# Two gated 3x3 convolutions: the three adding groups at lags of 0, 4 and 8 units instead of 0, 6 and 12

## The reference, cut to what matters

```python
# x: (16, 64, 56, 56) float32; w_a, w_b: (64, 64, 3, 3)
def qconv_cg(x, w, theta):
    base = cin // 4                       # 16 of the 64 channels
    yp = conv3x3(x[:, :base], w[:, :base])
    yr = conv3x3(x[:, base:], w[:, base:])
    d = jax.nn.sigmoid(2.0 * (yp - theta[None, :, None, None]))
    return yp + d * yr

h = jax.nn.relu(bn(qconv_cg(x, w_a, theta_a), gamma_a, beta_a, mean_a, var_a))
h = bn(qconv_cg(h, w_b, theta_b), gamma_b, beta_b, mean_b, var_b)
return jax.nn.relu(x + h)
```

## Time and profile before

| what | value |
|---|---|
| median of 3 runs | 432.99 us (432.92 to 433.02) |
| the profiled execution | 432.81 us, of which its span is 430.7 us |
| PE (matmuls) | 424.7 us busy, 99% of the span, 9248 matmuls |
| PE weight loads | 422.8 us, 98% |
| DVE | 294.8 us, 68% |
| ACT | 257.9 us, 60% |
| granted TensorE clock | 9 tenths or more in 39 of 40 slices, 7 in the last |
| DMA | 27.77 MB, 64 GB/s mean |

### The profile page before, as it was taken

How to read it: one execution, slowest core, us unless ns; L and a number is a source line. 1 busy time by engine, 2 the same in 40 slices (tenths; PEclk the granted TensorE clock), 3 DMA queues, 4 the chain that set the end, 5 groups by cost and what they waited for, 6 DMA issues and landing times.

```text
span 430.7 us, 20664 instructions
## 1 busy us (share of the span) xinstructions
PE 424.7 (99%) x9248; PEld 422.8 (98%) x9248; DVE 294.8 (68%) x609; ACT 257.9 (60%) x507; POOL 31.5 (7%) x93
## 2 busy tenths in 40 slices
PE   9999999999999999999999999999999999999995
PEld 8999999999999999999999999999999999999994
DVE  5798665867667867666876766776766786764555
ACT  5776556655657655666665566665565765564333
POOL 6051000000000000000000000200000000000001
PEclk9999999999999999999999999999999999999997
DMA  8440116341414214151431511522515151111133
GB/s 164 91 94 9 27 27 124 65 94 29 96 41 96 56 38 96 22 113 42 85 68 23 104 29 36 112 47 56 98 24 112 40 110 34 29 22 40 38 73 76
DMA packets 120535, 27.77 MB, mean 64 GB/s; under 512 B 119936, under 2 KB 120448, under 8 KB 120448
## 3 DMA queue, kind: packets, MB, share of 16 engines
q1 hardware_dynamic: 117584, 25.87, 29.3%
q10 hardware_dynamic: 2544, 0.59, 0.6%
q0 software_dynamic: 320, 0.00, 0.0%
HBM read 13.60 MB, written 12.85 MB: 61 GB/s over the span
## 4 chain that ended last, share of the span: by engine, by line
PE 98%; DVE 1%; ACT 1%; issue 0%; DVEq 0%
PE acc L526 96%; PE acc L482 1%; PE acc L553 0%; DVE rows_out L900 0%; ACT rows_out L698 0%; DVE mix L852 0%; ACT mix L673 0%; ACT z L684 0%; DVE rows_out L939 0%; DVEq L851 0%
## 5 line engine op out<-in xcount | busy, mean ns | idle before, releaser
L526 PE MATMUL acc<-x_lo,w_hi 32*128 32x392 f32 (+1 forms) x1536 | 255.4, 336 | 0.0
L526 PE MATMUL acc<-x_hi,w_hi 32*128 32x392 f32 (+1 forms) x1536 | 255.4, 336 | 0.0
L526 PE MATMUL acc<-x_hi,w_lo 32*128 32x392 f32 (+1 forms) x1536 | 255.3, 336 | 0.0
L526 PE MATMUL acc<-h_lo,w_hi 32*128 32x398 f32 (+2 forms) x1488 | 252.3, 339 | 0.0
L526 PE MATMUL acc<-h_hi,w_hi 32*128 32x398 f32 (+2 forms) x1488 | 251.5, 338 | 0.0
L526 PE MATMUL acc<-h_hi,w_lo 32*128 32x398 f32 (+2 forms) x1488 | 251.5, 338 | 0.0
L526 PEld LDWEIGHTS acc<-x_lo,w_hi 32*128 32x128 f32 x1536 | 228.9, 183 | 0.0
L526 PEld LDWEIGHTS acc<-x_hi,w_hi 32*128 32x128 f32 x1536 | 228.7, 183 | 0.1
L526 PEld LDWEIGHTS acc<-x_hi,w_lo 32*128 32x128 f32 x1536 | 228.8, 183 | 0.0
L526 PEld LDWEIGHTS acc<-h_lo,w_hi 32*128 32x128 f32 x1488 | 220.9, 183 | 0.2
L526 PEld LDWEIGHTS acc<-h_hi,w_hi 32*128 32x128 f32 x1488 | 220.8, 183 | 0.0
(11 more groups left out here) (85 smaller groups left out, 239.4 us busy)
## 6 DMA issues: line engine op xcount, KB each, us to landing
x<-in_x_dram SPq DMA_DIRECT2D x28, 392.0 KB, 5.4
out_dram<-rows_out SPq DMA_DIRECT2D x84, 98.0 KB, 2.5
out_dram<-rows_out SPq DMA_DIRECT2D x27, 84.0 KB, 2.3
out_dram<-rows_out SPq DMA_DIRECT2D x12, 126.0 KB, 2.9
x<-in_x_dram SPq DMA_DIRECT2D x5, 98.0 KB, 3.3
x_edge<-in_x_dram SPq DMA_DIRECT2D x4, 112.0 KB, 4.7
out_dram<-rows_out SPq DMA_DIRECT2D x3, 112.0 KB, 2.3
x<-in_x_dram SPq DMA_DIRECT2D x1, 294.0 KB, 4.4
```

Source lines behind the costliest of these rows:

```text
L526: return pe.matmul(sums(bank, blk), w[g * ROWS:(g + 1) * ROWS, tap], moving(blk, part, c, dx, g), start=(u == 0 and (alone or g == bank_gr ...
```

## The change

One constant. `begins` then starts group 2's visits 4 steps after group 1's, and group 3's 8 steps after. Group 1 (lag 0) and group 0 (lag 2) keep their steps. The order of the groups at each bank stays the same.

```diff
-OFFSET = (2, 0, 6, 12)
+OFFSET = (2, 0, 4, 8)
```

## The result

| | median | range of the runs | ratio to before |
|---|---|---|---|
| before | 432.93 us (20 runs) | 432.5 to 433.2 | |
| lags 0, 4, 8 | 433.54 us (20 runs) | 433.31 to 433.71 | 1.0015 [1.0009, 1.0021] |

The change makes the kernel 0.61 us slower. The interval doesn't contain 1, but the difference is smaller than the 0.2% set beforehand as the bound, so it counts as within it. The forecast was 433.4.

The account below looks back on a forecast made before the run. PE's stream of matmul units was taken to bound the kernel; start and bank +0.77 us, steps saved at the end -0.35, together +0.42, gave 433.4 us, range 432.6 to 434.8.

Parts of the forecast that it names:

- the bank's term: Second round: block 6's first unit waits for block 1's bank until 21.50 us, making the stream 0.77 us late, start included.
- group 0's extra delay: At the start group 0 loses 0.45 us, group 1 0.27; the additional 0.18 was taken as made good.
- The rounds: Steady rounds: each takes one group's own sum, 72 units of about 0.18 us, so lags don't enter without late waits.
- The start: First units of groups 2 and 3 wait for x_hi chunks until 7.10 and 7.95 us: group 0 +0.45, group 1 +0.27.
- Parameters and block 1's bank: First round: parameters' product at step 24 comes 0.45 us later, moving the second `gated`'s end from 20.82 to 21.27 us.
- Later takeovers: Later rounds, block's first unit waiting for `gated`: four steps take 0.72 of 1.09 us room, 0.37 left, nothing lost.
- Handovers: Next group's first unit at a bank: room falls from 0.69 to 0.33 us; cost taken as 0, bounds 0 and 0.4.
- the rival of a loss in each round: Handovers of groups 2 and 3 cost in the 14 rounds with a 342-column block: 436 to 440 us, chance 0.1.
- The end: `last_base` no longer waits behind `finish(124)`: 0.35 of 0.72 us gained, then group 0's last matmul holds it.
- The cheap start: Rival at the start: waits or parameters' chain have slack, stream 0 to 0.32 us late, 432.6 to 433.0; chance 0.2.
- The case of 434.0: Rival: one-off losses, start at its upper bound 0.95 and handovers 0.4 us in rounds 2 to 6; chance 0.17.
- The strict order: Rival on PE: each unit lasts as long as its longest matmul, so fewer wide steps gain, 432.3 us; chance 0.03.

Follow-up runs that it names:

- At 3 units: Lags 0, 3 and 8 in place of the 0, 6 and 12 of the kernel before: 434.30 against 432.98 us, ratio 1.0032.
- (0, 0, 4, 8): The changed kernel (lags 0, 4, 8) with group 0 at lag 0, not 2: 433.52 us, against 432.98 for the kernel before.
- the earlier parameters: The changed kernel (lags 0, 4, 8) with the parameters' product at step 20, not 24: 433.14 us, against 432.98 for the kernel before.

## Why the prediction was right, step by step

**Forecast +0.42 us on the profiled execution, measured +0.5 of its span, +0.61 of the medians.** The sum held, its size in part by luck: the bank's term was too large and group 0's extra delay was left out, and the two errors cancel.

- *The rounds.* Forecast: the lags don't enter a round's time. The first `gated` of rounds 13, 14 and 15 are 12.98 and 12.56 us apart (191.24, 204.22, 216.78), as in the earlier trace rows within 0.04. Right.
- *The start* was about right in size. Chunks 1 and 2 were ready at 6.84 and 7.62 us, and PE's next matmuls stand at 6.90 and about 7.7, where I had 7.10 and 7.95. Of this 0.03 and 0.10 is the chunks' earlier arrival; the rest is the weight load of 0.18, which the rows don't show in full between a release and the next matmul. By the gates, the first round lost 0.28, not 0.45. That is in the main the execution's own: 12.35 to 12.43 us behind a chunk that is ready at 7.72, as in the kernel before, the gate would stand at 20.07 to 20.15, 0.38 to 0.46 late. That other groups stand behind the wait was right, as PEld shows (two loads, 0.33 us idle, released by x_hi):

```profile
6.89 0.18 PEld L526 LDWEIGHTS acc<-x_hi,w_hi 32*128 32x128 f32 x2 [0.33 <-ACT x_hi L629]
```

- *Parameters and block 1's bank.* The chain was right in each link, but moved by the smaller start: L791 came at 10.88 us where I had 11.1, the second `gated` ended at 21.02, not 21.27, and the first matmuls came at 21.17, not 21.50.
- *Group 1's step 81* was forecast 0.77 late, and from there the whole stream. Groups 1, 2 and 3 came 0.55 to 0.58 late (group 3's visits, four steps earlier, end 0.14 us sooner: 0.72 - 0.14 = 0.58). The 0.2 us too many are mostly the 0.25 by which the second `gated` ended sooner than forecast (21.02, not 21.27). The extra 0.18 of group 0, which I took as made good, mostly wasn't: group 0 is 0.86 late behind the second round and 0.74 at the end, and the end hangs on group 0. So 0.77 was right for it by luck, within the bounds of 0.32 and 0.95.
- *Later takeovers.* No recurring cost at 4, 8. The room before was not 1.09 us: in round 14 group 3's load stood at 206.75 us, where the prediction had 207.20. After, it stands at 206.61, 0.41 behind the second `gated`'s end at 206.20; one that waits stands 0.12 behind, so 0.29 us are left, where I had 0.37. The two steps from 8 to 6 are 0.36, and there the takeover waits in each of the rounds 6 to 19.
- *Handovers.* Taken as 0 at 4 units, since only a lead is lost. They do wait there, 36 of 192, and only the last round shows a loss by the gates, 0.14 us, whose cause stays open. At 3 units the room would be 3 x 0.18 - 0.39 = 0.15 us; 0.59 us are lost over 95 blocks, but two rounds in the middle still take 25.54 us. So the rival of a loss in each round had the wait right and its price wrong.
- *The end.* `last_base` was forecast at 424.27 and came at 424.23 us, directly behind group 0's last matmul; `gated(127)` at 426.05 and came at 426.11. Of the cover of 0.35 us 0.26 was gained, by the gates of blocks 126 and 127. What I missed is that group 1 and block 125 hold the same end. `finish(125)` now starts 0.71 us after `last_base`, before 0.63, so this took up to 0.08 us here; and it made the expectation for (0, 0, 4, 8) wrong.
- *The first `gated` of round 14* was forecast at 204.41 and came at 204.22 us, inside the 204.0 to 205 set for it. With the 0.58 of group 3 in place of 0.77 the sum of the prediction, 204.36 - 0.72 + 0.58, gives it.
- *The other rivals.* The cheap start (432.6 to 433.0) falls with the 0.73 us at 32.76. The case of 434.0 needed 0.4 us from handovers in rounds 2 to 6, and by the gates nothing was lost there (0.73 late behind the second round, 0.60 at block 31). The strict order would have given 432.3; the Trainium skill (TensorE: Matmul & The Clock Gate, The mechanism) has matmuls of different tiles start and end strictly in program order, and the trace after disagrees, as before. On PE near the end:

```profile
423.20 0.36 PE L526 MATMUL acc<-e_lo,w_edge_hi 32*128 32x456 f32 x1
...
423.39 0.31 PE L526 MATMUL acc<-h_lo,w_hi 32*128 32x342 f32 x1
423.41 0.37 PE L526 MATMUL acc<-e_lo,w_edge_hi 32*128 32x456 f32 x1
423.55 0.31 PE L526 MATMUL acc<-h_lo,w_hi 32*128 32x342 f32 x1
```

The group on 342 columns starts every 0.16 us (423.39, 423.55), the one on 456 every 0.21 (423.20, 423.41): each at its own pace.

What stays open is a gain from the change. With the bank's cost taken away by the earlier parameters the time is +0.16 us and not measurably under the kernel before; and no kernel here was. The wait for the chunks at the start costs more than the 0.26 us that the end gives.

## What to carry to other kernels

Tightening the stagger of a pipelined schedule pays only at its two ends, and each end has its own partner: at the front the input that the now earlier unit needs, at the back the streams that were not moved. Before shortening a lag, list for each wait behind it how late its releaser already is, in steps, and look at the first round by itself, since set-up work there makes the same wait tighter than in the steady rounds. A wait that begins to hold a unit in the middle isn't yet a cost: where groups slide against each other, it can take a lead that the next round gives back. So measure over a whole period of the schedule (here two rounds), and not over the one round that grew.

## What the runs showed of the hardware

- A weight load that waits for a semaphore holds back the other row tiles' units too: at 21.17 us all four groups start within 0.01 us after a gap, though only one of them waited for the bank. The product of the parameters does the same at step 20, for 0.38 us.
- The load of a unit that waited for a bank starts 0.12 us after DVE's `gated` ends (21.02 to 21.14, 207.77 to 207.89). One that waited for an input alone starts 0.05 us after ACT (6.84 to 6.89).
- After a release, matmuls are recorded sooner than the end of the released weight load: 0.15 us after `gated`'s end at 21.02, with loads of 0.18 us. These first matmuls last 0.41 to 0.44 us, where one lasts 0.34 elsewhere, so their starts are too early by about 0.1. One that needs the exact moment of a release should use the ends or the next step.
- At 4 units between the end of one tile's visit and the next tile's first unit at the same bank, 36 of 192 first units waited for it; at 5 units none did (the closest load was 0.15 us behind the release), and at 6 none (0.31).
